# Attention and mixture of experts on one core: values stored without their ones, and two sets of buffers for the parts of queries and keys

## What is computed

```
x = x + attention(layernorm(x))
qkv = xn @ W_qkv + b_qkv                 # 256 -> 3 * 256
scores = q @ k.T * scale, causal          # for each batch and head, 512 x 512
out = softmax(scores) @ v                 # 16 channels a head
attention = out @ W_out + b_out
x = x + moe(layernorm(x))                 # gate, top 2 of 8, gelu(x @ w1) @ w2
```

## Time and profile before

| | before |
|---|---|
| median of 3 runs | 1096.27 us (1094.32 to 1097.19) |
| profiled execution: time, span | 1091.03 us, 1089.1 us |
| busy: PE, PEld, DVE, ACT, POOL | 911.5, 598.0, 731.8, 596.7, 471.4 us |
| mean granted clock of TensorE | 0.887 of full speed |
| bytes moved by DMA | 144.22 MB |

### The profile page before, as it was taken

The page is one execution under the profiler, slowest core; times in us unless marked ns, Lnnn a source line. Parts: engine busy times, 40 slices in busy tenths (PEclk is TensorE's granted clock), DMA queues, the critical chain, the costliest instruction groups (busy, mean ns, idle before and its releaser), DMA issues.

```text
span 1089.1 us, 21658 instructions
## 1 busy us (share of the span) xinstructions
PE 911.5 (84%) x7052; PEld 598.0 (55%) x7052; DVE 731.8 (67%) x1632; ACT 596.7 (55%) x1085; POOL 471.4 (43%) x536
## 2 busy tenths in 40 slices
PE   4788868775878787888887898879988999999995
PEld 2444423222242323333332787768877898989894
DVE  6353688775648798887883686766756676767663
ACT  2554537563747677766766564444634454545451
POOL 2000003323424565646565557454564555455542
PEclk9898988887678887879785999989999999999998
DMA  9887757764665757575735552232322333332322
GB/s 208 266 287 247 257 191 221 227 160 112 187 205 153 212 158 201 144 212 137 196 86 164 180 114 41 42 84 41 46 42 46 55 46 55 46 55 45 56 45 25
DMA packets 150568, 144.22 MB, mean 132 GB/s; under 512 B 42112, under 2 KB 128896, under 8 KB 150336
## 3 DMA queue, kind: packets, MB, share of 16 engines
q1 hardware_dynamic: 117856, 97.92, 31.4%
q0 software_dynamic: 17024, 20.81, 11.9%
q10 hardware_dynamic: 15584, 24.12, 6.9%
HBM read 88.44 MB, written 54.10 MB: 131 GB/s over the span
## 4 chain that ended last, share of the span: by engine, by line
PE 38%; DMA 17%; issue 11%; DVE 10%; SPq 7%; POOL 7%; ACT 6%; DVEq 2%; ACTq 0%; POOLq 0%
PE banks L729 13%; PE banks L713 13%; DMA qk_parts<-weights 4%; DMA arena<-in_L_ffn_w 4%; SPq L1779 3%; POOL slot_tokens L1556 3%; PE banks L635 2%; PE banks L592 2%; PE banks L647 2%; POOL out L1600 2%; DMA weighed_values<-arena 1%; DVE arena L1160 1%; DMA late_weights<-arena 1%; SPq L1766 1%; PE banks L577 1%
## 5 line engine op out<-in xcount | busy, mean ns | idle before, releaser
L935 ACT ACTIVATE arena<-banks,arena 128x256 f32<-128x256 f32 x312 | 158.9, 561 | 197.9 <-issue 130.3
L729 PE MATMUL banks<-weights,arena 128*128 x1872 | 217.0, 275 | 9.0 <-DVE arena L1419 8.9
L713 PE MATMUL banks<-arena,weights 128*128 128x256 f16 x1872 | 213.1, 274 | 3.9 <-DMA weights<-late_weights 3.0
L1600 POOL DMA_INDIRECT out<-arena x78 | 128.0, 1641 | 202.5 <-DVE arena L1430 101.2
L729 PEld LDWEIGHTS banks<-weights,arena 128*128 128x128 f16 x1872 | 183.8, 99 | 34.6 <-issue 12.1
L713 PEld LDWEIGHTS banks<-arena,weights 128*128 x1872 | 183.7, 98 | 27.2 <-issue 4.9
L592 PE MATMUL banks<-arena 50*128 50x128 f16 (+3 forms) x512 | 125.7, 352 | 36.2 <-ACT arena L862 13.9
L564 PE MATMUL banks<-arena 48*128 48x128 f16 (+3 forms) x512 | 103.2, 345 | 34.8 <-DVE arena L1158 25.9
L1419 DVE SCALAR_TENSOR_TENSOR arena<-arena 128x512 f16<-128x512 f32 x156 | 119.3, 765 | 5.6
L592 PEld LDWEIGHTS banks<-arena 50*128 50x128 f16 x512 | 38.2, 102 | 147.1 <-issue 52.7
L1417 DVE TENSOR_SCALAR arena<-arena 128x512 f16<-128x512 f32 x156 | 78.2, 501 | 58.4 <-ACT arena L935 56.9
(11 more groups left out here) (172 smaller groups left out, 1373.7 us busy)
## 6 DMA issues: line engine op xcount, KB each, us to landing
weights<-in_L_ffn_w ACTq DMA_DIRECT2D x16, 1024.0 KB, 9.1
arena<-in_L_ffn_w SPq DMA_DIRECT2D x32, 512.0 KB, 5.3
qk_parts<-weights SPq DMA_DIRECT2D x96, 128.0 KB
arena<-qk_parts SPq DMA_DIRECT2D x128, 96.0 KB, 3.4
v_rows<-weights SPq DMA_DIRECT2D x8, 1024.0 KB, 9.6
weighed_values<-arena SPq DMA_DIRECT2D x32, 256.0 KB
token_rows<-arena SPq DMA_DIRECT2D x12, 512.0 KB, 5.5
weights<-in_L_attn_x ACTq DMA_DIRECT2D x8, 512.0 KB, 8.9
```

The lines of the kernel that those rows point to most:

```text
L713: m = pe.matmul(bank[:, c * TILE:(c + 1) * TILE], w1[:, k, wp, f:f + P], xp[:, k, :], start=(i == 0), stop=(i == len(terms) - 1))
L729: m = pe.matmul(bank[:, c * D:(c + 1) * D], hp[:, f, c * P:(c + 1) * P], w2[:, f // (FC // 2), wp, f % (FC // 2), :], start=(f == 0 and i ...
L935: m = act.activation(h_32[r % 2][:, c, :], banks[:, 1 + c2, c * TILE:(c + 1) * TILE], ACT.Gelu, bias=b1_now[j % 2][:, 2 * c2 + c:2 * c2 + ...
L1600: g.indirect_dma_start(acc_dram[:, :], bass.IndirectOffsetOnAxis(slot_of(j, c), 0), y[j % 2][:, c, :], None, compute_op=ALU.add).then_inc( ...
```

## The change

1. `v_dram` has 16 columns a head in place of 32, and `v_out` the values alone. The bias addition writes the values of a group of four heads with the channel outside and the head inside (`(g d h)`), so that the four values of one channel lie beside each other.
2. `load_v` loads only the values, 64 columns of `v_blocks[u % 2]`, for each of four tiles of tokens. The other 64 columns are ones, set once: in the buffer of odd units at the start, in that of even units after the maxima of the last two experts' weights are known. The first `weigh` waits for `ones_set`.
3. `weigh` takes its stationary columns from both halves with a step of four elements, `v_blocks[u % 2][:, kt, h:V_WIDE:HG]`.
4. `qk_part` has two sets, b % 2, with a semaphore for each. ScalarE waits at L813 for the stores of batch b - 2, where it waited for those of b - 1.

```diff
-        v_dram = dram("v_rows", (B, T, H, 2 * HD), F32)
+        v_dram = dram("v_rows", (B, T, H, HD), F32)
...
-        v_one = [area.take(TT * HG * 2 * HD, t=TT, h=HG, d=2 * HD) for area in (lent, a2)]
+        V_WIDE, V_LEN = 2 * HG * HD, TT * 2 * HG * HD
+        v_one = [area.take(V_LEN) for area in (lent, a2)]
+        v_blocks = [x[:, 0:TT * V_WIDE].rearrange("p (t d) -> p t d", t=TT) for x in v_one]
...
-        qk_part = [a1.take(2 * T // 2, F16, s=2, t=T) for _ in range(2 * KC)]
-        v_out = a1.take(2 * TT * D, t=TT, h=H, d=2 * HD)
+        qk_part = [[a1.take(2 * T // 2, F16, s=2, t=T) for _ in range(2 * KC)] for _ in range(2)]
+        v_out = a1.take(TT * D, t=TT, d=D)
...
+        def qk_stored(c, b):
+            return sem(f"qk_store{c}_{b % 2}"), 48 * (b // 2 + 1)
+        def v_and_ones(u, kt, h):
+            return v_blocks[u % 2][:, kt, h:V_WIDE:HG]
...
                 if kt == W_ORDER[0]:
+                    w.wait_ge(sem("ones_set"), 1)
...
-                    m = pe.matmul(banks[32 * h:32 * h + 32, O_BANK, kt * P:T], v_one[u % 2][:, kt, h, :],
+                    m = pe.matmul(banks[32 * h:32 * h + 32, O_BANK, kt * P:T], v_and_ones(u, kt, h),
...
-                    if b > 0:
-                        w.wait_ge(sem(f"qk_store{c}"), 48 * b)
+                    if b >= 2:
+                        w.wait_ge(*qk_stored(c, b - 2))
...
-                    v.tensor_tensor(v_out[:, 2 * half:2 * half + 2, :, 0:HD],
+                    v.tensor_tensor(
+                        v_out[:, 2 * half:2 * half + 2, :].rearrange("p s (g d h) -> p s g h d", g=NG, h=HG),
...
+            g.memset(v_blocks[1][:, :, HG * HD:V_WIDE], 1.0)
             for s in range(4):
-                g.memset(k_st[s], float(2 ** SHIFT))
-            g.memset(v_out[:, :, :, HD:2 * HD], 1.0).then_inc(sem("memory_set"), 1)
+                m = g.memset(k_st[s], float(2 ** SHIFT))
+            m.then_inc(sem("memory_set"), 1)
+            w.wait_ge(sem("tops"), 2 * LATE)
+            g.memset(v_blocks[0][:, :, HG * HD:V_WIDE], 1.0).then_inc(sem("ones_set"), 1)
...
-                sp.dma_start(v_one[u % 2].rearrange("p t h d -> p t (h d)"),
+                sp.dma_start(v_blocks[u % 2][:, :, 0:HG * HD],
```

More of the change, by code:

```diff
@@ L177, in build @@
         p_T = [area.take(HG * PT_LEN, h=HG, c=PT_LEN) for area in (lent, a2)]
-        v_one = [area.take(TT * HG * 2 * HD, t=TT, h=HG, d=2 * HD) for area in (lent, a2)]
-        LENT = -(-(HG * PT_LEN + TT * HG * 2 * HD) // HALF)
+        V_WIDE, V_LEN = 2 * HG * HD, TT * 2 * HG * HD
+        v_one = [area.take(V_LEN) for area in (lent, a2)]
+        v_blocks = [x[:, 0:TT * V_WIDE].rearrange("p (t d) -> p t d", t=TT) for x in v_one]
+        LENT = -(-(HG * PT_LEN + V_LEN) // HALF)
         assert LENT == late_dram.shape[0] and LENT * HALF == 3 * EW // 2
@@ L810, in project @@
                     w.wait_ge(sem("qk_made"), number + 1)
-                    if b > 0:
-                        w.wait_ge(sem(f"qk_store{c}"), 48 * b)
-                    act.activation(qk_part[c][:, 0, :], banks[:, 5 + c % 2, :], ACT.Identity, bias=b_qk[:, c:c + 1],
+                    if b >= 2:
+                        w.wait_ge(*qk_stored(c, b - 2))
+                    act.activation(qk_part[b % 2][c][:, 0, :], banks[:, 5 + c % 2, :], ACT.Identity, bias=b_qk[:, c:c + 1],
                                    scale=scale)
@@ L986, in scalar @@
                     for c in range(2 * KC):
-                        w.wait_ge(sem(f"qk_store{c}"), 48 * B)
+                        w.wait_ge(*qk_stored(c, B - 2))
+                        w.wait_ge(*qk_stored(c, B - 1))
                     w.wait_ge(sem("v_store"), 16 * B)
@@ L1091, in project @@
                         w.wait_ge(sem("v_store"), 16 * b)
-                    v.tensor_tensor(v_out[:, 2 * half:2 * half + 2, :, 0:HD],
-                                    banks[:, (4, 7)[half], :].rearrange("p (s h d) -> p s h d", s=2, h=H),
-                                    b_v.rearrange("p (h d) -> p h d", h=H).unsqueeze(1).broadcast_to([P, 2, H, HD]),
-                                    ALU.add).then_inc(sem("v_added"), 1)
+                    v.tensor_tensor(
+                        v_out[:, 2 * half:2 * half + 2, :].rearrange("p s (g d h) -> p s g h d", g=NG, h=HG),
+                        banks[:, (4, 7)[half], :].rearrange("p (s g h d) -> p s g h d", s=2, g=NG, h=HG),
+                        b_v.rearrange("p (g h d) -> p g h d", g=NG, h=HG).unsqueeze(1).broadcast_to(
+                            [P, 2, NG, HG, HD]), ALU.add).then_inc(sem("v_added"), 1)
                 for c in range(2 * KC):
@@ L1103, in project @@
                     w.wait_ge(sem("qk_full"), number + 1)
-                    both(qk_part[c][:, 1, :], qk_full[number % 2], qk_part[c][:, 0, :], ALU.subtract).then_inc(
+                    both(qk_part[b % 2][c][:, 1, :], qk_full[number % 2], qk_part[b % 2][c][:, 0, :], ALU.subtract).then_inc(
                         sem("qk_low"), 1)
@@ L1669, in load_unit @@
                 w.wait_ge(sem("memory_set"), 1)
-                w.wait_ge(sem(f"qk_store{g // 2}"), 48 * (b + 1))
-                w.wait_ge(sem(f"qk_store{KC + g // 2}"), 48 * (b + 1))
+                w.wait_ge(*qk_stored(g // 2, b))
+                w.wait_ge(*qk_stored(KC + g // 2, b))
                 for j in range(PAIR):
@@ L1684, in load_v @@
                 w.wait_ge(sem("tops"), 2 * LATE)
-                sp.dma_start(v_one[u % 2].rearrange("p t h d -> p t (h d)"),
+                sp.dma_start(v_blocks[u % 2][:, :, 0:HG * HD],
                              v_dram[b].rearrange("(t p) h d -> p t (h d)", p=P)[
-                                 :, :, g * HG * 2 * HD:(g + 1) * HG * 2 * HD]).then_inc(sem(f"v_in{u % 2}"), 16)
+                                 :, :, g * HG * HD:(g + 1) * HG * HD]).then_inc(sem(f"v_in{u % 2}"), 16)
             def keep_o(u):
@@ L1774, in sync @@
                         sp.dma_start(v_dram[b].rearrange("(t p) h d -> p t (h d)", p=P),
-                                     v_out.rearrange("p t h d -> p t (h d)")).then_inc(sem("v_store"), 16)
+                                     v_out).then_inc(sem("v_store"), 16)
                     w.wait_ge(sem("qk_low"), 2 * KC * b + c + 1)
@@ L1778, in sync @@
                     for block, part in enumerate(((0, 1, 0), (0, 0, 1))[which]):
-                        sp.dma_start(qk_dram[which, b, head:head + P // HD, block, :, :], qk_part[c][:, part, :]).then_inc(
-                            sem(f"qk_store{c}"), 16)
+                        sp.dma_start(qk_dram[which, b, head:head + P // HD, block, :, :], qk_part[b % 2][c][:, part, :]).then_inc(
+                            qk_stored(c, b)[0], 16)
                     if (b, c) == (B - 1, 2):
```

## The result

The changed kernel takes 1070.78 us (median of 4 runs, 1070.13 to 1072.76), the kernel before 1096.73 us (1094.32 to 1097.45). The ratio is 0.977, 95% interval 0.975 to 0.979: 26 us faster, where 19 were forecast, inside the range. The profiled execution went from 1091.03 to 1071.05 us.

A forecast was written before the change was run, and what follows sets the result against it. A loop of part stores and L813 bounds the projection, with SyncE and DMA near their own bound. -16.9 - 3.2 - 2 + 3 = -19 us on 1091.03 gives 1072 profiled, 1077 median; range 1069 to 1083, 8 in 10 1062 to 1091.

The forecast's parts named there:

- ScalarE's 47.8 us of waits go, and they are not the gain: Projection, L813: waits for stores of parts vanish with the second set; SyncE with the transfers is late next.
- Batches 1 to 5: 16.9 us, by the rate of the best batch: Projection: 20.1 MB at the best batch's 294 GB/s take 68.4 us in place of 85.3, gaining 16.9 us.
- the 9.7 us of the average rate: Projection, batches 1 to 5: 20.1 MB at the average 266 GB/s take 75.6 us, a gain of 9.7 us.
- the first rival: Projection: the wait moves to the single value buffer, or only bytes count; 1087 us, chance 0.20.
- Its signs: Projection: L1092 waits longer for its store; batches stay above 15 us with L813's wait gone.
- Batches 6 and 7: 3.2 us: End of projection, 42.2 us before the first score product: at most 10.3 us to be had, a third taken.
- L1092 counted at nothing, at most 4 us: VectorE's bias addition with 16-byte steps: up to 1.29 us more a batch, nothing counted, at most 4 us showing.
- The stationary columns: +3 us: Weight loads of `weigh` in attention: 16-byte steps cost 39 us, mostly beside matmuls, so 3 us slower.
- the slow loads: Rival in attention's `weigh`: each strided load takes 114 ns more, +39 us on the path; 1113 us, chance 0.10.
- The loads of values in attention: -2 us: Attention: 4.2 MB less share queues with weight loads; bounds 0 and 12 us, 2 us gain taken.
- The median: Whole kernel: median of the runs lies 5.2 us above the profiled execution, so 1077 us forecast.
- TensorE's floor: Projection, batches 1 to 5: 5 x 11.20 = 56.0 us, a gain of 29.3; as a rival 1061 us, chance 0.12.

The follow-up runs named there:

- fourth stores of 128 and of 4 KB: Changed kernel plus a fourth store for each block: with 128 KB 1109.65 us, ratio 0.9946; with 4 KB 1098.56 us, 0.990.
- the pair on one chip: Kernel before and changed kernel, both unchanged, traced again on the same chip: 1111.91 us (ratio 1.0008) and 1095.68 us (0.9856).
- first pair: First measurement of the changed kernel against the kernel before, chip not known: 1070.78 against 1096.73 us, ratio 0.977.

## Why the prediction was right, and where its reasons were not

The forecast of the profiled time, 1072 us, was met (1071.05), but by errors that cancelled. The sum had 19.1 us and the spans differ by 20.2. Against it batches 1 to 5 gave 4.9 us less, batches 6 and 7 gave 2.5 more, attention 6.0 more, the experts lost 2.1, and the projection began 0.4 later. The closeness of the sum is luck.

*ScalarE's 47.8 us of waits go, and they are not the gain.* Right: no wait at L826 for stores is left, and without the second set the stage ends no later. What was late next, though, was VectorE at the single value buffer, with 16.6 us of waits, and not SyncE: with two value buffers or the store on ScalarE's queue the batches fall to 62.9 and 65.3 us. The bytes act on the stage (fourth stores of 128 and of 4 KB) in part through how long the store of the values takes.

*Batches 1 to 5: 16.9 us, by the rate of the best batch.* This step failed. "With the loop open SyncE always has a store to issue" was to raise the rate from 266 to 294 GB/s; it stayed at 264. The loop was not open, since VectorE still waited for the store of the values; and where it was, with two value buffers, the rate was 271 GB/s, still not 294. The five batches took 73.3 us, a gain of 12.0, not 16.9. It is the 9.7 us of the average rate, with 2.3 more because 3.4 MB less, not 2.6, fell into these windows. The second set brought nothing to this stage: alone it ends at 155.1 against 154.9 us, and without it the stage ends at 140.3 us. So the first rival (only the bytes count, and the wait goes to the single value buffer) had the mechanism, though not the time: it named 1087 us, and its floor of some 15 us a batch did not hold (12.65 and 14.41 us in batches 3 and 4). Its signs were in the trace: VectorE's wait grew from 14.9 to 16.6 us, the DMA share of batches 3 and 4 was 0.79 and 0.80, not near 0.9, and batches 1 and 5 stayed above 15 us with L813's wait gone.

*Batches 6 and 7: 3.2 us.* Mis-sized: 42.2 us became 36.5, a gain of 5.8. The store of the values is smaller there too, and the nine stores ahead of the top rows took 5.86 us where they took 10.00:

```profile
143.94 10.00 SPq L1779 DMA_DIRECT2D qk_parts<-weights  x9
```

```profile
130.69 5.86 SPq L1798 DMA_DIRECT2D qk_parts<-weights  x9
```

With the 12.0 us this gives 17.7 us, against 20.1 in the sum, two errors that partly cancelled. In the pair on one chip the two parts gave 6.6 and 3.3 us.

*L1092 counted at nothing, at most 4 us.* The instruction took 57% longer (1,071 ns against 681), within the bound, and the run without the step shows nothing in the projection.

*The stationary columns: +3 us.* The load went from 119 to 147 ns, 28 ns more, where 38 was estimated and 64 was the point from which the slow loads decide. The measured cost on the path is not told from 0, and the slow case did not come. By the rule of the Trainium skill ("SBUF — State Buffer", section on the DMA port swizzle) at least two accesses must hit one line of 16 bytes for full bandwidth, so that a step of 16 bytes should cost something. The trace agrees, with 28 ns a load; that this makes the slow case and a loss, as the prediction drew from it, it does not show.

*The loads of values in attention: -2 us.* The first pair shows 5.0 us less in attention, the pair on one chip 7.1 us more, where the spread within one kernel is 13 us and goes with the granted clock. This term stays open.

*The median.* The forecast added 5.2 us to the profiled time for the median, and the changed kernel showed no such distance, so that 1070.78 us were measured where 1077 were forecast. The gain is 26 us in the first pair of medians and 15 to 18 us on chips 4 and 5. Why they differ is not settled; the granted clock in attention and in the experts was lower in the later traces.

## What to carry to other kernels

When a stage waits in turn for several buffers of one stream of transfers, compare the bytes moved per us in the batches with and without the waits before counting a second buffer as a gain: here a second set for the parts moved the wait from ScalarE to VectorE, and the stage kept its end. Then look at what ends the stage: a second value buffer brought the early batches near TensorE's floor, and more than half of that was given back waiting for one transfer that the same queue issues behind the stores. A cheap test is to put back the bytes alone or the issues alone; with one value buffer that separated them in one pair of runs. Bytes that carry constants (half of each value row here) are worth taking out first.

## What the runs showed of the hardware

- An addition from PSUM and SBUF to SBUF with 512 float32 elements takes 681 ns when it writes in order, and 1,071 ns when its innermost step is 16 bytes in the same pattern of four dimensions: 0.76 ns more for each element.
- A weight load of 32 float32 columns takes 119 to 124 ns side by side and 147 ns with 16 bytes between their starts, while its time on the path stayed out of sight.
- In the projection, stores and loads together ran at 253 to 273 GB/s from 32 to 136 us in every version, at a DMA share of 0.76 to 0.81, while single batches reached 302 GB/s and a share of 0.90. What holds the mean there is not shown; neither the count of issues nor a move of one store to ScalarE's queue changed it much.
- A store of 4 KB in rows of 32 bytes holds SyncE for 0.46 to 1.23 us, 0.57 in the median, where the shortest issues of 128 KB took 0.56. The 32 more issues still left the end of the stage where it was (144.2 us against 144.3).
- The same two kernels differed by 26 us in the first pair of medians and by 15 to 18 us on chips 4 and 5. Attention of one kernel took 443.5, 448.7 and 462.1 us at granted clocks of 0.79, 0.77 and 0.75.
